# A rebuilt cross-product stage, and a base product in two halves, in a decoder layer on one NeuronCore

## What is computed

```python
x = x + attention(layernorm(x))            # 32 heads of 128, rms norm of q and k over all heads
x = x + cross(layernorm(x), ctx)
x = x + ffn(layernorm(x))

def fake_quant(v, scale, zp):              # cross: both operands quantised, then a plain product
    return (clip(round(v / scale + zp), 0, 255) - zp) * scale
cross = fake_quant(x1, s1, z1) @ fake_quant(ctx, s2, z2)

base = x3 @ base_W.T + base_b              # ffn
probs = softmax(x3 @ router_W.T + router_b)            # 15 columns
w = top-8 probabilities, summed by expert map into 8 experts
lora = ((x3 @ A.T) * w) @ B * 2.0          # 8 experts of rank 16
ffn = base + lora
```

## Time and profile before

| what | us |
|---|---|
| device time, timed runs | 538.88, 539.81, 539.90 |
| device time of the profiled execution | 538.6 |
| its span | 536.7 |
| TensorE busy in the span | 522.3 (97%) |
| ScalarE, VectorE, GpSimd busy | 355.9, 331.2, 271.1 |
| span's part behind the last head (from 494.6) | 42.1 |

### The profile page before, as it was taken

One profiled execution on the slowest core, in us unless ns is written; L12 is line 12 of the kernel. 1 busy time (PEld: TensorE's weight loads), 2 busy tenths in 40 slices (PEclk: granted clock), 3 DMA queues, 4 the chain that ended last, 5 costly groups with the idle time before them and its releaser, 6 DMA issues.

```text
span 536.7 us, 9733 instructions
## 1 busy us (share of the span) xinstructions
PE 522.3 (97%) x3211; PEld 461.4 (86%) x3213; DVE 331.2 (62%) x696; ACT 355.9 (66%) x745; POOL 271.1 (51%) x229
## 2 busy tenths in 40 slices
PE   6999999999999999999999999999999999998897
PEld 5888888878888889999999999999999999986486
DVE  6254444276666677666667666666766666666655
ACT  3666666656666767777677677767767776775740
POOL 3344444364455545655646465564646556465340
PEclk9999999999999999999999999999999999999999
DMA  5444634223333222111221221212242311220002
GB/s 182 138 137 152 219 98 163 92 79 98 98 98 98 59 81 60 59 45 55 59 59 59 59 59 42 56 58 59 59 121 69 126 44 58 60 79 20 2 0 80
DMA packets 23496, 43.43 MB, mean 81 GB/s; under 512 B 3633, under 2 KB 3889, under 8 KB 23217
## 3 DMA queue, kind: packets, MB, share of 16 engines
q1 hardware_dynamic: 23472, 43.13, 26.5%
HBM read 41.03 MB, written 2.10 MB: 80 GB/s over the span
## 4 chain that ended last, share of the span: by engine, by line
PE 90%; DVE 5%; ACT 2%; DMA 1%; POOL 1%; issue 0%; SPq 0%; DVEq 0%
PE p_t L496 5%; PE p_v L575 5%; PE p_v L577 5%; PE p_t L497 5%; PE p_o L496 5%; PE p_v L576 5%; PE p_o L497 5%; PE p_o L499 5%; PE p_t L499 5%; PE acc L594 5%; PE acc L595 5%; PE acc L596 5%; PE p_t L561 5%; PE p_o L613 3%; PE p_o L615 3%; PE p_o L614 3%
## 5 line engine op out<-in xcount | busy, mean ns | idle before, releaser
L1090 DVE TENSOR_TENSOR w_lo<-raw,w_hi 128x512 fp32r<-128x512 f32 x64 | 44.2, 691 | 77.2 <-ACT w_hi L705 77.1
L957 POOL TENSOR_TENSOR wo_lo<-raw,wo_hi 128x512 fp32r<-128x512 f32 x31 | 40.1, 1293 | 100.5 <-ACT wo_hi L839 100.5
L705 ACT CAST w_hi<-raw 128x512 fp32r<-128x512 f32 x64 | 39.9, 623 | 68.0 <-PE p_t L499 30.3
L774 ACT ACTIVATE probs<-p_s,nbias,rq_t 128x256 f32<-128x256 f32 x128 | 71.3, 562 | 19.1 <-DVE nbias L1192 19.1
L575 PE MATMUL p_v<-w_hi,xnt_hi 128*128 128x256 f32 x256 | 77.2, 301 | 0.0
L577 PE MATMUL p_v<-w_hi,xnt_lo 128*128 128x256 f32 x256 | 72.3, 283 | 0.0
L576 PE MATMUL p_v<-w_lo,xnt_hi 128*128 128x256 f32 x256 | 72.2, 282 | 0.0
L939 POOL TENSOR_TENSOR acc_k<-acc_k,square 128x512 f32<-128x512 f32 x32 | 41.6, 1301 | 52.5 <-ACT square L720 52.5
L939 POOL TENSOR_TENSOR acc_q<-acc_q,square 128x512 f32<-128x512 f32 x32 | 43.5, 1359 | 40.3 <-ACT square L720 40.0
L823 ACT CAST pt_hi<-p_t 128x512 fp32r<-128x512 f32 x64 | 37.4, 584 | 38.8 <-PE p_t L561 38.8
L957 POOL TENSOR_TENSOR w_lo<-raw,w_hi 128x512 fp32r<-128x512 f32 x32 | 44.8, 1399 | 20.6 <-ACT w_hi L757 20.6
(11 more groups left out here) (276 smaller groups left out, 1486.2 us busy)
## 6 DMA issues: line engine op xcount, KB each, us to landing
raw<-in_wv SPq DMA_DIRECT2D x36, 256.0 KB, 2.6
raw<-in_wk SPq DMA_DIRECT2D x32, 256.0 KB, 2.6
raw<-in_wq SPq DMA_DIRECT2D x32, 256.0 KB, 2.5
raw<-in_wo SPq DMA_DIRECT2D x31, 256.0 KB, 2.6
ctx_f<-in_ctx SPq DMA_DIRECT2D x4, 512.0 KB, 3.6
xin<-in_x SPq DMA_DIRECT2D x4, 256.0 KB, 3.5
xb<-in_x SPq DMA_DIRECT2D x4, 256.0 KB, 5.9
ctx_kept<-ctx_k SPq DMA_DIRECT2D x1, 1024.0 KB, 5.0
```

The costliest lines, as they stand in the source:

```text
L774: act.activation(probs[:, b, a, :], p_s[:, a, :], ACT.Exp, bias=nbias[:, b, a:a + 1], scale=rq_t[:, 2 * b + a:2 * b + a + 1], accum_out=rs ...
L957: pool.tensor_tensor(dst, raw[:, slot, :], hi, ALU.subtract).then_inc(w_lo_pool, 1)
L1090: dve.tensor_tensor(w_lo[:, n, 0:NC * DH], raw[:, r, :], w_hi[:, n, 0:NC * DH], ALU.subtract).then_inc(w_lo_dve, 1)
```

## The change

In the cross stage:
- The column part is split into `corr_hi` (ScalarE) and `corr_lo` (VectorE, new `column_lo`), and each tile adds both by two fp32r identity matmuls in place of one fp32 matmul. The constant of the row part is left out of it. The column sums of element 0 go to `p_t`, those of element 1 to `p_s`; before, it was the other way round.
- `linear` uses Relu, which is the lower clip. `quantise` is one instruction a tile (upper clip, add the rounding number) in place of `xn`, in fp32. The transposes are of fp32, and ScalarE's copy back takes the rounding number off by a bias.
- ScalarE keeps x1 with the column part in `x_res` (`keep_x1`, as soon as TensorE has added it), and `second_sum` is one VectorE instruction: product times scale plus `x_res`. `scaled` is gone.
- The row sums of all tiles are 16 one-column matmuls in one run (`row_sums`), into `p_flat[3]`, between `transpose_x3(0)` and `transpose_x3(1)`. The row part is added to the output in the last VectorE instructions, which so have three operands.
- The orders of all three engines' lists are rewritten.

Behind it, `base_out(0)` is done as two chunks of its contraction ahead of `transpose_x3(2)` and two behind it, and `transpose_x3(3)` comes ahead of `low_rank(1)`.

The diff, cut to its core:

```diff
@@ column_sums, add_column_part, transpose_q1, quant_product
-                mm = pe.matmul(p_flat[1 + b], ones_b[:], ctx_q[:, b * NC + c, :], start=(c == 0), stop=(c == NC - 1))
+                mm = pe.matmul(p_flat[2 - b], ones_b[:], ctx_q[:, b * NC + c, :], start=(c == 0), stop=(c == NC - 1))
         def add_column_part(pe, t):
+            if t % 2 == 0:
+                pe.wait_ge(col_lo_done, t // 2 + 1)
             pe.wait_ge(linear_done, t + 1)
-            pe.matmul(acc[t][:], ident[:], corr[:, t // 2, :], start=False, stop=True, skip_group_check=True)
+            pe.matmul(acc[t][:], ident_r[:], corr_hi[:, t // 2, :], start=False, stop=False, skip_group_check=True)
+            pe.matmul(acc[t][:], ident_r[:], corr_lo[:, t // 2, :], start=False, stop=True, skip_group_check=True
+                      ).then_inc(col_part_added, 1)
         def transpose_q1(pe, t):
             pe.wait_ge(q1_done, t + 1)
             if t >= 2:
-                pe.wait_ge(scaled_done, t - 1)
+                pe.wait_ge(q1t_out, t - 1)
             for c in range(NC):
-                mm = pe.transpose(p_flat[2 + t % 2].bitcast(BF16)[:, c * P:(c + 1) * P],
-                                  q1[:, t, c * P:(c + 1) * P], ident_b[:])
+                mm = pe.transpose(p_flat[2 + t % 2][:, c * P:(c + 1) * P], xn[:, t, c * P:(c + 1) * P], ident[:])
         def quant_product(pe, t):
             pe.wait_ge(q1t_out, t + 1)
+            if t >= 2:
+                pe.wait_ge(x2_done, t - 1)
+            elif t == 1:
+                pe.wait_ge(col_lo_done, 2)
...
+        def row_sums(pe):
+            for t in range(NT):
+                for c in range(NC):
+                    mm = pe.matmul(p_flat[3][:, t:t + 1], q1t[:, t, c, :], ones_b[:, 0:1],
+                                   start=(c == 0), stop=(c == NC - 1))
+            mm.then_inc(row_sums_ready, 1)
@@ base_out
+            if t < 2:
+                pe.wait_ge(x2_done, 3 + t)
+            elif t == 3:
+                pe.wait_ge(row_part_done, 1)
@@ TensorE's list
             transpose_q1(pe, 2)
+            add_column_part(pe, 3)
             transpose_q1(pe, 3)
-            add_column_part(pe, 3)
             quant_product(pe, 2)
             quant_product(pe, 3)
             transpose_x3(pe, 0)
+            row_sums(pe)
             transpose_x3(pe, 1)
             low_rank(pe, 0)
-            base_out(pe, 0)
+            base_out(pe, 0, range(0, 2))
             transpose_x3(pe, 2)
+            base_out(pe, 0, range(2, NC))
+            transpose_x3(pe, 3)
             low_rank(pe, 1)
-            transpose_x3(pe, 3)
             low_rank(pe, 2)
@@ ScalarE
-                act.activation(corr[:, b, :], p_flat[1 + b], ACT.Identity, scale=qc[:, 3:4], bias=qc[:, 6:7]
+                act.activation(corr_hi[:, b, :], p_flat[2 - b], ACT.Copy, scale=qc[:, 3:4]
-                act.activation(xn[:, t, :], acc[t][:], ACT.Identity, scale=cs[:, t:t + 1], bias=cb[:, t:t + 1]
+                act.activation(xn[:, t, :], acc[t][:], ACT.Relu, scale=cs[:, t:t + 1], bias=cb[:, t:t + 1]
+            def keep_x1(t):
+                act.wait_ge(col_part_added, t + 1)
+                act.copy(x_res[:, t, :], acc[t][:]).then_inc(x1_kept, 1)
-                act.copy(q1t[:, t, :, :].rearrange("p c n -> p (c n)"), p_flat[2 + t % 2].bitcast(BF16)[:, 0:D]
-                         ).then_inc(q1t_out, 1)
-            def scaled(t):
...
+                act.activation(q1t[:, t, :, :].rearrange("p c n -> p (c n)"), p_flat[2 + t % 2], ACT.Identity,
+                               bias=qc[:, 7:8]).then_inc(q1t_out, 1)
@@ VectorE
+            def quantise(t):
+                dve.wait_ge(linear_done, t + 1)
+                dve.tensor_scalar(xn[:, t, :], xn[:, t, :], QMAX, ROUND, ALU.min, ALU.add).then_inc(q1_done, 1)
             def second_sum(t):
-                dve.wait_ge(scaled_done, t + 1)
-                dve.tensor_tensor(x_res[:, t, :], acc[t][:], xn[:, t, :], ALU.add).then_inc(x2_done, 1)
+                dve.wait_ge(x1_kept, t + 1)
+                dve.wait_ge(product_ready, t + 1)
+                dve.scalar_tensor_tensor(out=x_res[:, t, :], in0=p_flat[t % 2], scalar=qc[:, 2:3],
+                                         in1=x_res[:, t, :], op0=ALU.mult, op1=ALU.add).then_inc(x2_done, 1)
+            def column_lo(b):
+                dve.wait_ge(col_part_done, b + 1)
+                dve.scalar_tensor_tensor(out=corr_lo[:, b, :], in0=p_flat[2 - b], scalar=qc[:, 3:4],
+                                         in1=corr_hi[:, b, :], op0=ALU.mult, op1=ALU.subtract
+                                         ).then_inc(col_lo_done, 1)
+            def row_part():
+                dve.wait_ge(row_sums_ready, 1)
+                dve.tensor_scalar(rsd[:], p_flat[3][:, 0:NT], qc[:, 5:6], qc[:, 6:7], ALU.mult, ALU.add
+                                  ).then_inc(row_part_done, 1)
...
-                dve.tensor_tensor(xn[:, t, cols], y, x_res[:, t, cols], ALU.add
-                                  ).then_inc(out_done, 1)
+                dve.scalar_tensor_tensor(out=xn[:, t, cols], in0=y, scalar=rsd[:, t:t + 1],
+                                         in1=x_res[:, t, cols], op0=ALU.add, op1=ALU.add).then_inc(out_done, 1)
```

More of the change, by code:

```diff
@@ L45 @@
 QMIN, QMAX = 0.0, 255.0
+assert QMIN == 0.0
 U1 = 2 * NH
@@ L97, in decoder_layer @@
         ident_r = here("ident_r", [P, P], F32R)
-        ident_b = here("ident_b", [P, P], BF16)
         ones = here("ones", [P, P], F32)
@@ L147, in decoder_layer @@
         xn = here("xn", [P, NT, D], F32, q_at)
-        q1 = here("q1", [P, NT, D], BF16, q_at + 4 * KS)
         q1t = here("q1t", [P, NT, NC, P], BF16, q_at + 6 * KS)
-        corr = here("corr", [P, B, SKV], F32, q_at + 8 * KS)
+        corr_hi = here("corr_hi", [P, B, SKV], F32R, q_at + 8 * KS)
+        corr_lo = here("corr_lo", [P, B, SKV], F32R, q_at + 4 * KS)
         hw = here("hw", [P, NT, P], F32, q_at + 10 * KS)
@@ L263, in decoder_layer @@
         product_ready = sem("product_ready")
-        scaled_done = sem("scaled_done")
+        col_lo_done = sem("col_lo_done")
+        col_part_added = sem("col_part_added")
+        x1_kept = sem("x1_kept")
+        row_sums_ready = sem("row_sums_ready")
         x2_done = sem("x2_done")
@@ L426, in quant_product @@
             pe.wait_ge(q1t_out, t + 1)
+            if t >= 2:
+                pe.wait_ge(x2_done, t - 1)
+            elif t == 1:
+                pe.wait_ge(col_lo_done, 2)
             for c in range(NC):
[L428 to L432, removed]
-            mm.then_inc(product_ready, 1)
+                mm = pe.matmul(p_flat[t % 2], q1t[:, t, c, :], ctx_q[:, t // 2 * NC + c, :], start=(c == 0),
+                               stop=(c == NC - 1))
+            mm.then_inc(product_ready, 1)
+        def row_sums(pe):
[4 more added lines that the diff above has]
+            mm.then_inc(row_sums_ready, 1)
         def transpose_x3(pe, t):
@@ L454, in low_rank, with base_out @@
             mm.then_inc(low_rank_ready, 1)
-        def base_out(pe, t):
+        def base_out(pe, t, chunks=range(NC)):
             tt = slice(t * P, (t + 1) * P)
-            if t == 0:
+            if t == 0 and chunks[0] == 0:
                 pe.wait_ge(w_lo_pool, NS - 1)
-                pe.wait_ge(scaled_done, NT)
+            if t < 2:
+                pe.wait_ge(x2_done, 3 + t)
+            elif t == 3:
+                pe.wait_ge(row_part_done, 1)
             if t < NT - 1:
@@ L466, in base_out @@
             for dst, g in groups:
-                for c in range(NC):
+                for c in chunks:
                     hi, lo = [w[:, g, c * PW:(c + 1) * PW] for w in (w_hi, w_lo)]
@@ L888, in x3_hi @@
                          ).then_inc(x3_hi_done, 1)
[L890 to L899, removed]
+            linear(0)
+            linear(1)
+            keep_x1(0)
+            keep_x1(1)
+            q1_out(0)
+            q1_out(1)
+            linear(2)
+            linear(3)
+            keep_x1(2)
+            q1_out(2)
+            q1_out(3)
             normalise(0)
-            scaled(2)
+            keep_x1(3)
             x3_hi(0)
             normalise(1)
-            scaled(3)
             x3_hi(1)
@@ L1297, in pair_coefficients @@
                 dve.tensor_scalar(cb[:, a], cm[:, a], -1.0, qs_b[:, 1:2], ALU.mult, ALU.add).then_inc(coef_ready, 1)
[L1299 to L1312, removed]
-            def second_sum(t):
-                dve.wait_ge(scaled_done, t + 1)
-                dve.tensor_tensor(x_res[:, t, :], acc[t][:], xn[:, t, :], ALU.add).then_inc(x2_done, 1)
+            def quantise(t):
+                dve.wait_ge(linear_done, t + 1)
+                dve.tensor_scalar(xn[:, t, :], xn[:, t, :], QMAX, ROUND, ALU.min, ALU.add).then_inc(q1_done, 1)
+            def second_sum(t):
+                dve.wait_ge(x1_kept, t + 1)
[11 more added lines that the diff above has]
+                                  ).then_inc(row_part_done, 1)
```

(19 more changed lines are left out.)

10 lines of the change are left out of this document (1 added, 9 removed).

## The result

The changed kernel took 536.46 us (median of six runs, 535.55 to 537.59), the kernel before 539.86 over its six: ratio of the measurement 0.9948, 95% interval 0.993 to 0.9966 (the two medians alone would give 0.9937). A second measurement on one chip gave 536.53 against 539.27, ratio 0.9949 (0.9932 to 0.9966). So it is faster by 2.7 us (the ratios) to 3.4 us (the first pair of medians), half a per cent; 2.2 were forecast.

What follows compares the result with a forecast made beforehand. Behind the last head a latency chain over several engines, then TensorE's block, then the router on VectorE bound the kernel. Gains 2.1 + 0.25 - 0.13 = 2.2 us gave 537.6 from 539.8, range 536.7 to 539.3.

Steps and rivals of the forecast that it cites:

- The sum: Work behind the last head, followed with priced durations: 2.1 + 0.25 - 0.13 = 2.2 us faster.
- The rival that spread the gain over hand-overs: Some 12 hand-overs on the path, 0 to 0.1 us more each: gain only 1.0, 538.8; chance 0.13.
- tile 3 waits for VectorE: In the cross stage, VectorE does statistics 0 before quantise 3, done at 504.92; transposes of tile 3 ready 505.66.
- The block: TensorE from transposes of x3 tile 1 to the router: 0.3 us of waits vanish, end 519.1 instead of 521.18.
- The router: Its subtraction no longer runs beside POOL's base-bias additions, which end before the router: 0.25 us gained.
- The tail: Last VectorE additions take three operands and end 0.2 late; through the fourth store 0.13 us is lost.
- Row sums: 16 pairs of load and matmul on TensorE before transposes of x3 tile 1: 1.3 us, hidden in 1.6.
- my lower bound of 0.7: Low end of 0.7 to 1.4 us for the 16 row-sum pairs, from loads 0.045 apart in bf16 transposes.
- The rival with 0.26 a pair: Row-sum matmuls not overlapped with their loads: run of 4.1 us, gain gone, 540.1; chance 0.05.
- Relu: Rival in ScalarE's `linear`: Relu needs another function table, four loads of 1.28 us, 2.9 slower, 542.7; chance 0.04.
- The slow sums: Rival: VectorE's three-operand sums take 0.94 us, delaying quantise 3 and the tail; gain 1.2, 538.6; chance 0.07.
- The clock: Rival: lighter stage lowers the clock; transposes, products and split matmuls at half speed cost about 3, 540.4; chance 0.03.

Runs made afterwards that it cites:

- late-POOL kernel: Changed kernel with POOL's four base-bias additions held until the last low-rank product; router 7.8 us instead of 5.64, end of span 43.33 instead of 39.68.
- padded twin: Changed kernel with an unused 128 x 128 bf16 buffer in place of the removed one, so later SBUF buffers lie as before; 536.40 us.

## Why the prediction was right

*The sum, step by step.* With the 1.27 us between the two executions' starts of the stage taken off, the hand-followed times against the trace are: column part 499.24 and 499.23, last copy of x1 done 501.12 and 501.17, product 0 at 501.80 and 501.81, quantise 3 done 504.92 and 504.97, `normalise(0)` 506.25 and 506.30, `normalise(1)` 508.44 and 508.46, transposes of tile 1 509.31 and 509.32. That this works to 0.05 us has one reason: nearly every duration had a row of the same operation with the same places of operands, and every hand-over was taken from the chain. The rival that spread the gain over hand-overs had priced 0 to 0.1 us more for each of twelve; they cost nothing more.

Two things besides were not as told. The sum prices the stage and what follows, 2.2 against 2.4 measured there, and between executions with a granted clock of 0.999 or more the timed gain was 2.2 as well; the excess up to 2.7 or 3.4 has no term in it, and the median of 536.46 lies in the range only by way of the ratio. And where the prediction says that tile 3 waits for VectorE, the chain has TensorE's queue: the transposes of tile 3 start at 506.33, less 1.27 is 505.06, and VectorE was done at 504.97. The two ways were equally long to 0.1 us, so naming the wrong one cost nothing here; that is luck.

*The block* gave 0.43 instead of 0.3: 9.66 us from its first transposes to the logits, 10.09 before. Without the halves it gives 0.13, so 0.3 of it are the halves. The prediction's own subtraction leaves 0.34 of waits, rounded to 0.3; the remaining 0.1 lies in its prices: transposes behind other matmuls held the queue for 0.36, not 0.41, and the three low-rank products in a row took 4.06 us, not 4.14.

*The router* gave 0.26 (5.90 to 5.64), forecast 0.25, and the late-POOL kernel shows its cause. *The tail* lost 0.09, forecast 0.13.

*Row sums: the mis-sized term.* 16 pairs took 0.54 us, 0.025 a pair ((0.54 - 0.16) / 15), not 1.3; it lies even below my lower bound of 0.7. The price stood in the trace of before: four of the old matmuls, each 0.163 long, took 0.24 in all, 0.026 apart. I had read the loads instead (0.36 for four), of which the first was done 0.2 us ahead while the product still ran, and for the lower bound loads that each had a transpose of 128 columns behind them. The rival with 0.26 a pair could have been struck out by the same row. The error cost nothing because there was 1.6 us of room. Placed on the path, they cost 0.44.

*Relu* needed no table load: the changed kernel's trace has one load, 1.28 us, as before. The slow sums didn't come about (752 ns). *The clock* rival, at 0.03, was priced for the changed kernel and didn't show behind the last head in its three profiles (two executions of it and one of its padded twin), but it did in two variants, in the block and not in the stage, for 1.6 us and not 3. The stage's granted clock of 1.00 in one execution was poor evidence against it.

*The remainder.* The part behind the last head explains 2.4 of the 2.7 to 3.4 us. On the chip where both kernels' clocks are listed, the rest goes with runs of the kernel before in which the granted clock fell; whether the change makes those rarer stays open.

## What to carry to other kernels

Where a stage is a chain over several engines, follow it by hand with the durations of rows that have the same operand places, each engine's own order, and the hand-overs of the chain itself; then ask of every reordering who is late next, for the same edit gained 0.3 us or lost 1.05 us depending on how early `normalise(2)` came. TensorE's waits can be filled with those parts of a split product that need only the high part. Keep GpSimd's long elementwise work away from chains of small VectorE operations with two SBUF operands.

## What the runs showed of the hardware that was not expected

- A load (bf16, 128x128) with a one-column matmul takes 0.025 us a pair in a run of 16, and 0.026 in the runs of four of the kernel before.
- A VectorE operation on 60 columns with two SBUF operands took up to 1.32 us beside GpSimd's 512-column additions, 0.23 alone, and ended some 0.1 us behind the end of one of these additions; operations with one tensor operand between them were not held, nor were the low parts, which read one of two from PSUM (0.69 beside POOL).
- The granted clock fell to half for 3.3 us although TensorE had been at work for 1.9 us by then, in two of the profiles and not in others of nearly the same stage. In the first 20 us a mean of 0.74 over six us goes with a start 1.13 us longer in the same kernel (495.90 against 494.77).
